# A vision transformer block on one core: token weights loaded and folded chunk by chunk

## What is computed

```python
x5 = jnp.concatenate([x] + _shifts(x), axis=-1)
tokens = _patchify(x5, PATCH)
mu = jnp.mean(tokens, axis=-1, keepdims=True)
var = jnp.mean(jnp.square(tokens - mu), axis=-1, keepdims=True)
ln = (tokens - mu) * jax.lax.rsqrt(var + EPS) * gamma + beta
return jnp.einsum('bnf,fd->bnd', ln, W) + b
```

## Time and profile before

| | us |
|---|---|
| median of 3 runs | 690.59 (689.09 to 691.2) |
| profiled execution, its own time | 694.64 |
| its span, first to last instruction | 692.8 |
| TensorE busy | 656.4 (95%) |
| VectorE busy | 496.1 (72%) |
| ScalarE busy | 385.5 (56%) |
| POOL busy | 106.5 (15%) |

### The profile page before, as it was taken

How to read it: one execution, slowest core, us unless ns; L and a number is a source line. 1 busy time by engine, 2 the same in 40 slices (tenths; PEclk the granted TensorE clock), 3 DMA queues, 4 the chain that set the end, 5 groups by cost and what they waited for, 6 DMA issues and landing times.

```text
span 692.8 us, 29942 instructions
## 1 busy us (share of the span) xinstructions
PE 656.4 (95%) x13218; PEld 574.3 (83%) x13218; DVE 496.1 (72%) x1351; ACT 385.5 (56%) x1045; POOL 106.5 (15%) x328
## 2 busy tenths in 40 slices
PE   4878999999999999999999998899999999999998
PEld 2667888888888888888888787688999999999997
DVE  5566878888888888888888986576557547556644
ACT  0245776766776776676676766744444444444442
POOL 1212123223212312312312400110000000000000
PEclk9988999999999999999999999999999999999999
DMA  8792121111111111111100000000000000000000
GB/s 310 260 286 82 35 65 34 35 64 35 36 63 35 50 48 35 52 47 35 34 4 5 4 4 4 4 1 2 0 24 1 1 0 24 2 1 23 1 1 23
DMA packets 13425, 30.64 MB, mean 44 GB/s; under 512 B 1264, under 2 KB 7536, under 8 KB 13040
## 3 DMA queue, kind: packets, MB, share of 16 engines
q1 hardware_dynamic: 13296, 28.73, 12.7%
HBM read 27.16 MB, written 1.57 MB: 41 GB/s over the span
## 4 chain that ended last, share of the span: by engine, by line
PE 87%; DVE 6%; ACT 3%; issue 2%; DMA 1%; SPq 1%; POOL 0%; DVEq 0%; POOLq 0%
PE ps L409 29%; PE ps L574 18%; PE ps L564 16%; PE ps L296 6%; PE ps L313 2%; PE ps L374 2%; PE ps L427 2%; PE ps L356 2%; PE ps L314 1%; PE ps L348 1%; DVE uu L857 1%; DVE se L813 1%; DVE sst L811 1%; PE ps L440 1%; PE ps L328 1%
## 5 line engine op out<-in xcount | busy, mean ns | idle before, releaser
L919 DVE SCALAR_TENSOR_TENSOR acc<-ps,comb,acc 128x192 f32<-128x192 f32 x256 | 89.1, 411 | 84.0 <-PE ps L574 83.9
L574 PE MATMUL ps<-w_sb,work 128*128 128x192 f32 x768 | 140.3, 326 | 0.7 <-ACT work L744 0.7
L574 PEld LDWEIGHTS ps<-w_sb,work 128*128 128x128 f32 x768 | 129.3, 189 | 9.0 <-issue 1.1
L744 ACT ACTIVATE work<-ps 128x512 f32<-128x512 f32 x96 | 57.3, 597 | 138.7 <-PE ps L564 138.7
L409 PEld LDWEIGHTS ps<-rr 64*64 64x64 f32 x3840 | 98.2, 135 | 20.3 <-issue 11.9
L409 PE MATMUL ps<-rr 64*64 64x64 f32 x3840 | 110.8, 223 | 4.0 <-issue 3.2
L409 PE MATMUL ps<-uu,qq 64*64 64x64 f32 x4608 | 99.4, 226 | 11.9 <-DVE uu L857 10.3
L857 DVE SCALAR_TENSOR_TENSOR uu<-rr,qq 128x384 f32<-128x384 f32 x160 | 86.5, 563 | 32.5 <-ACT qq L651 24.2
L409 PEld LDWEIGHTS ps<-uu,qq 64*64 64x64 f32 x4608 | 82.9, 135 | 29.5 <-DVE uu L857 19.1
L658 ACT ACTIVATE rr<-ps 128x384 f32<-128x384 f32 x160 | 73.8, 489 | 57.7 <-PE ps L409 57.3
L296 PE MATMUL ps<-weff,xtb 128*128 128x193 f32 x240 | 51.3, 351 | 1.1 <-DVE t L768 1.1
(11 more groups left out here) (142 smaller groups left out, 1070.0 us busy)
## 6 DMA issues: line engine op xcount, KB each, us to landing
xtb<-xt_dram SPq DMA_DIRECT2D x16, 512.0 KB, 3.8
work<-x_dram SPq DMA_DIRECT2D x16, 512.0 KB, 4.1
wsh<-ws_dram SPq DMA_DIRECT2D x10, 288.0 KB, 5.7
w_sb<-w_dram SPq DMA_DIRECT2D x1, 2304.0 KB, 22.3
w_a<-w_dram SPq DMA_DIRECT2D x1, 1536.0 KB, 10.5
w_b<-w_dram SPq DMA_DIRECT2D x2, 768.0 KB, 14.7
out_dram<-acc SPq DMA_DIRECT2D x3, 384.0 KB, 2.6
mult<-copies_dram SPq DMA_DIRECT2D x1, 512.0 KB, 8.2
```

Source lines behind the costliest of these rows:

```text
L574: last = pe.matmul(ps[:, 2 + 2 * (e % 2) + j // 2, (j % 2) * DIM:(j % 2 + 1) * DIM], hid[:, n % 4, j * P:(j + 1) * P], w2_sb[:, c, :], sta ...
L744: act.activation(hid[:, n % 4, :], ps[:, UPB[n % 3], :], ACT.Gelu_apprx_tanh).then_inc(gelu_done, 1)
L919: last = dve.scalar_tensor_tensor(out=a, in0=ps[:, 2 + 2 * (e % 2) + j // 2, (j % 2) * DIM:(j % 2 + 1) * DIM], scalar=comb[:, g * GT + j, ...
```

## The change

The same loads, folds and products are issued in another order, and the loads are cut otherwise. The weights lie in memory by chunk, then tap. Each chunk comes in two loads, taps 0 to 2 (288 KB) and taps 3 and 4 (192 KB), twelve in all; `whalo` comes behind chunk 1, `cst` behind chunk 2, `xt[0]` behind chunk 3. VectorE folds by the list `FOLD`, which keeps two chunks going at a time, and `whalo` behind the twelfth fold. TensorE runs beta's products of chunks 0 to 2, tile 0's products of chunks 0, 1, 6 and 7, beta's of chunk 3, then chunk by chunk the tokens with column sums between, and beta's products of chunks 4 and 5 and of `whalo` behind them.

```diff
+FOLD = sorted(((c, f) for c in range(6) for f in range(5)), key=lambda a: 2.5 * a[0] + a[1])
+TOKS = (0, 1, 6, 7, 2, 3, 4, 5)
+def folds(c, f):
+    n = FOLD.index((c, f))
+    return n + 1 + 2 * (n >= 12)
...
-            def taps(half, f0, f1):
-                for f in range(f0, f1):
-                    sp.dma_start(wsh[:, half, f], ws[:, half, f]).then_inc(tap_loaded[half][f], 16)
+            def taps(c):
+                for part, f in enumerate((slice(0, 3), slice(3, 5))):
+                    sp.dma_start(wsh[:, c, f], ws[:, c, f]).then_inc(taps_loaded[c][part], 16)
...
-            taps(0, 0, 5)
-            taps(1, 0, 3)
+            taps(0)
+            taps(1)
+            sp.dma_start(whalo[:], wh).then_inc(halo_loaded, 16)
+            taps(2)
             sp.dma_start(cst[:], const).then_inc(const_loaded, 16)
+            taps(3)
             sp.dma_start(xtb[:, 0], xt[0]).then_inc(xt_loaded[0], 16)
-            taps(1, 3, 5)
-            sp.dma_start(whalo[:], wh).then_inc(halo_loaded, 16)
+            taps(4)
+            taps(5)
...
-            def beta(n, w):
-                z = 32 * (n % 4)
+            def beta(m, n, w):
+                z = 32 * (m % 4)
...
+            def first_tok(c):
+                pe.wait_ge(folded, 14 if c >= 6 else folds(c, 4))
+                last = pe.matmul(C[:, 0:DIM + 1], xtb[:, 0, c, :], weff[:, c, :], start=(c == TOKS[0]), stop=(c == TOKS[-1]))
+                if c == TOKS[-1]:
                     last.then_inc(tok_done, 1)
...
+            def column_sum(c):
+                z = 32 * (c % 4)
+                return pe.matmul(D[z:z + 32, 0:DIM], ones[:, 0:32], weff[:, c, 0:DIM], start=(c < 4), stop=(c >= 4),
+                                 tile_position=(0, z))
...
-            beta_taps(0)
+            beta_chunk(0)
+            beta_chunk(1)
+            beta_chunk(2)
             pe.wait_ge(mean_set, 1)
             pe.wait_ge(xt_loaded[0], 16)
-            first_tok(0, 3)
-            first_tok(3, 6)
-            first_tok(6, CH)
             pe.wait_ge(ones_set, 1)
-            column_sums()
-            beta_taps(1)
+            for c in (0, 1, 6, 7):
+                first_tok(c)
+            beta_chunk(3)
+            first_tok(2)
+            for c in (0, 1, 2, 6):
+                column_sum(c)
+            first_tok(3)
+            column_sum(3)
+            column_sum(7)
+            first_tok(4)
+            column_sum(4)
+            first_tok(5)
+            column_sum(5).then_inc(wsum_done, 1)
+            beta_chunk(4)
+            beta_chunk(5)
             pe.wait_ge(halo_loaded, 16)
-            beta(30, whalo[:, 0, :])
-            beta(31, whalo[:, 1, :]).then_inc(beta_done, 1)
+            beta(30, 30, whalo[:, 0, :])
+            beta(31, 31, whalo[:, 1, :]).then_inc(beta_done, 1)
...
+            for n, (c, f) in enumerate(FOLD):
+                if n == 12:
+                    dve.wait_ge(halo_loaded, 16)
+                    for b in range(2):
+                        dve.tensor_scalar(weff[:, 6 + b, 0:DIM], whalo[:, b, :], gbs[:, 0, 30 + b:31 + b], None,
+                                          ALU.mult).then_inc(folded, 1)
+                if f in (0, 3):
+                    dve.wait_ge(taps_loaded[c][f // 3], 16)
+                k = c // 3 * 15 + 3 * f + c % 3
+                g = gbs[:, 0, k:k + 1]
+                w = weff[:, c, 0:DIM]
+                if f == 0:
+                    dve.tensor_scalar(w, wsh[:, c, f, :], g, None, ALU.mult).then_inc(folded, 1)
+                else:
+                    dve.wait_ge(folded, folds(c, f - 1))
+                    dve.scalar_tensor_tensor(out=w, in0=wsh[:, c, f, :], scalar=g, in1=w,
+                                             op0=ALU.mult, op1=ALU.add).then_inc(folded, 1)
```

More of the change, by code:

```diff
@@ L122, in vit_block_kernel @@
         hid = work[:].rearrange("p (c n) -> p c n", c=4)
-        with nc.sbuf_tensor("wsh", [P, 2, 5, 3, DIM], F32) as wsh, nc.sbuf_tensor("whalo", [P, 2, DIM], F32) as whalo:
+        with nc.sbuf_tensor("wsh", [P, 6, 5, DIM], F32) as wsh, nc.sbuf_tensor("whalo", [P, 2, DIM], F32) as whalo:
             pass
@@ L144, in vit_block_kernel @@
             "const_loaded gamma_loaded halo_loaded tokb_loaded mult_loaded")
-        tap_loaded = [[sem(f"tap_loaded_{half}_{f}") for f in range(5)] for half in range(2)]
+        taps_loaded = [[sem(f"taps_loaded_{c}_{part}") for part in range(2)] for c in range(6)]
         x_loaded, xt_loaded = sems("x_even_loaded x_odd_loaded"), sems("xt_even_loaded xt_odd_loaded")
@@ L487, in iteration, with beta_chunk @@
                     second_window(k, t)
-            def beta(n, w):
-                z = 32 * (n % 4)
-                return pe.matmul(A[z:z + 32, 0:DIM], gbs[:, 1, n:n + 1].to_broadcast([P, 32]), w, start=(n < 4), stop=(n >= 28),
+            def beta(m, n, w):
+                z = 32 * (m % 4)
+                return pe.matmul(A[z:z + 32, 0:DIM], gbs[:, 1, n:n + 1].to_broadcast([P, 32]), w, start=(m < 4), stop=(m >= 28),
                                  tile_position=(0, z))
-            def beta_taps(half):
+            def beta_chunk(c):
@@ L495, in beta_taps @@
                 for f in range(5):
[L496 to L504, removed]
-                    last.then_inc(tok_done, 1)
@@ L507, in column_sums @@
[L507 to L512, removed]
+                    if f in (0, 3):
+                        pe.wait_ge(taps_loaded[c][f // 3], 16)
+                    beta(5 * c + f, c // 3 * 15 + 3 * f + c % 3, wsh[:, c, f, :])
@@ L1090 @@
     wsh, whalo = by_pixel(L0_tok_W)
+    wsh = wsh.transpose(0, 1, 3, 2, 4).reshape(P, 6, 5, DIM)
     gs, gh = by_pixel(L0_tok_gamma)
```

## The result

| | before | changed |
|---|---|---|
| median, 7 runs each | 691.18 us | 694.57 us (693.13 to 699.38) |
| profiled execution, its span | 692.8 | 691.5 |
| ratio | | 1.0071, 95% interval 1.0052 to 1.0091 |

The changed kernel is slower, by 3.6 to 6.3 us by the ratio's interval. A ratio is taken over all executions, so it can differ a little from the quotient of the two medians. One execution of that second timing took 1410.76 us, twice the others, and is left out. Forecast were 691.7 us and a range up to 693.6, so the direction was right and the size too small. The profiled executions alone would mislead: that of the kernel before (694.64 us) was 3.5 us over its median, that of the changed kernel (693.31) one of its fastest. So the starts are compared, not the spans.

A forecast was written before the change was run, and what follows sets the result against it. TensorE was taken to bound the kernel, nearly always busy from 61 to 470 us, with start delays shifting everything behind. Tile 0's end 1.45 us later, partly swallowed at tile 1, left +1.1: 690.6 + 1.1 = 691.7 us, range 689.0 to 693.6.

The forecast's parts named there:

- Loads: Weight and token loads at the start: xt[0] at 12.0 us, last chunk at 14.6, xt[1] unchanged at 22.6.
- Rival 3: Split loads at the start cost bandwidth: all parts 0.4 to 0.9 us later, +1.5 to +1.7, 692.2 us; chance 0.09.
- Folds: VectorE's folds at the start end at 17.2 us against 15.85 before, ahead of tile 0's last product.
- The floor: Tile 1 can't begin before xt[1] lands at 22.6 us, so the change can't give more than 0.6 us here.
- TensorE's order decides: TensorE's own queue bounds tile 0: six rounds of column sums instead of two, last product ending at 19.5 us.
- E: The time when tile 0's last product ends on TensorE: 18.05 us before, forecast 19.5, 1.45 later.
- Forward: The 1.45 us passes unchanged to tile 1's start (24.6 us); tile 1 ends +0.95 later, taken as +1.1.
- a sign of being wrong: Tile 1's products running at full clock throughout would show the forecast wrong; it had them low from 23.7 to 27.1 us.
- Rival 2: A longer low clock spell: all of tile 1 runs low, 5.1 us, giving 692.7 to 693.7 us; chance 0.17.
- Rival 1: TensorE's clock rises before about 14.5 us through denser work at the start: 689.5 or 688.4 us; chance 0.16.
- Rival 4: TensorE's order doesn't bind at the start: E stays near 18, within 0.3 us, 690.6 us; chance 0.12.

The follow-up runs named there:

- second timing: The unaltered changed kernel timed once more against the kernel before: 693.71 against 691.03 us, ratio 1.0045 (1.0024 to 1.0066).

## Why the prediction was right and wrong

- **Loads**: right. `xt[0]` at 12.1 (12.0 forecast), the first product at 12.22 (12.1; the view names `issue` and not a DMA as its releaser), the last chunk at 14.7 (14.6), `xt[1]` at 22.7 (22.6). The rule of the Trainium skill ("DMA: Bandwidth & Descriptors", section Bandwidth) to batch into large transfers didn't bite: 400 GB/s with the smaller loads, 401 before. Rival 3 fell: loads and folds alone gave 0.9997.
- **Folds**: right, 17.07 against 17.2, and beside the path, as said.
- **The floor** at `xt[1]`'s landing: right, seen when the tokens were put back in a block (released by its DMA at 23.27).
- **TensorE's order decides**: right in kind (sums behind the tokens again: 1.0012; strewn in the kernel before: 1.0096 and 1.0080). **This is the step that failed, by its size.** The term was priced as products of 0.34 and rounds of 0.33 at the full clock, as if blocks could be cut for nothing, and put E 1.45 us later; it came 2.10 later. The part of the queue that ran at the full clock, 15.99 to 20.15 us, holds four products and five rounds, 3.2 us by those prices with the tail of 0.15, and took 4.2. A lone token steps by 0.52 to 0.53 instead of 0.34 (four of them, with the last one's end: 0.8 us), the single sum by 0.44 instead of 0.33, the block of four by 0.78 and the pair by 0.77 instead of 0.66 (0.35 together). The Trainium skill ("TensorEngine Tiling (Array Packing)", section Key Properties) says that a change of the tiling mode drains TensorE. It states no price, but these steps and the pauses of the weight loads agree with it, and the forecast had left the rule out. How much of a step is the drain and how much the weight load that no longer runs beside the product ahead, no run separates. Against this loss the clock rose 1.4 us earlier here than in the trace before (beta's products fall from 517 to 326 ns near 15.4 us), which hid half of the miss: with a rise at 16.9, E would have come near 20.9 (an estimate: 1.4 us more at half the speed).
- **Forward**: that E passes unchanged to tile 1 was right (2.10 us at E, 2.11 at tile 1). That tile 1's own low clock swallows a part of it, 1.1 left of 1.45, was wrong. In the first trace tile 1 took 4.53 us as before and the transposes began 2.12 us later (29.66 against 27.54). In five of the eight it ran wholly at the full clock (2.86 us), which the prediction had named as a sign of being wrong; two of the three traces before did so too. Over all traces the start costs 2.05 us, and a pure delay of that kind cost 2.15 us in the median. So +1.1 should have been +2.
- **The rest of the loss** is not explained. The medians rose by 3.4 and 2.7 us in the two timings, the ratios stand for 4.9 and 3.1. The lower eleven of the 18 executions have their median 2 us over the kernel before, as the start says; the other seven stand 5 to 8 us over it. Rival 2, all of tile 1 at the low clock, was seen once, in the trace with the sums in free quarters and at 5.49 us for tile 1, over its price of 5.1; in the changed kernel's eight traces it never happened.
- **Rival 1** (the clock rises before 14.5 us) didn't happen: by the durations the first rise lay between 15.2 and 17.8 us in the eight traces. The three earliest, 15.2 to 15.4, had tile 1 at 25.13 to 25.28, since TensorE's queue and never the folds set E. **Rival 4** fell with the first row.
- The range was to end with rival 2, which by its own sum ends at 693.7 and not 693.6; the measured median lies above both.

What stays open: what the changed kernel's upper group is; why the strewn kernel before loses more (4.6 and 6.1 us in the medians) than the changed one with the same start; and the scatter behind the start, which no run here was made to explain.

## What to carry to other kernels

On TensorE, count the switches between full-width and quarter-width products, not only the products: block work by width, and let neighbouring narrow products take different quarters. Work that nobody waits for yet (the column sums) belongs behind the product that others wait for, even if its inputs are there. Before a sum rests on where the clock rises, look at three traces instead of one, and try a suspected delay by itself: two dead memsets told what one microsecond at the start is worth. And before a late start is called the cause of a slow execution, look at one that started late: the strewn kernel's trace that began tile 1 3.7 us later took 1.2 us less than its sister.

## What was not expected of the hardware

- A full-width product of two instructions between narrow ones takes a step of 0.52 to 0.53 us at the full clock, 0.34 in a row of its like. Its weights, 0.19 us an instruction, load beside the product ahead in such a row, and behind narrow products they start with their own product, whose first record is then 431 ns instead of 327. In reverse, a lone narrow product costs 0.44 where a round of four costs 0.33. At the low clock a token and a single sum take 1.72 us together, at the full clock 0.97.
- TensorE's clock can stay low while the rows show no idle time. The middle trace of the sums strewn in the kernel before shows it busy for all of both stretches (length, then PE busy; the clock column reads 1.00 there, but the durations above, 527 ns, tell that the level was the low one, 1.2 GHz):

```profile
16.00:20.00 4.00, 4.00 (x15) 1.56 (x14) 0.00 (x0) 0.00 (x0) 0.00 (x0) 1.00 0.92 321
20.00:24.00 4.00, 4.00 (x20) 1.70 (x22) 0.16 (x1) 0.46 (x1) 0.00 (x0) 1.00 0.39 157
```

  The Trainium skill ("TensorE: Matmul & The Clock Gate", section Why this matters for your kernels) tells to keep TensorE busy without a gap to get and hold the full clock. By that this start should have had it. The record of busy time doesn't bear it out here, and no run of this case tells why.
- In one and the same program the first rise of the clock moves: between 15.2 and 17.8 us in eight traces of the changed kernel, near 18.2, 18.6 and 26.7 in three of the sums strewn in the kernel before, where it moved tile 1 by up to 3.7 us.
